# ViT block on one core: values per token tile through DRAM, masked keys, unrolled attention with block-diagonal values

## What is computed

```
x = layernorm(patches, ln1) ; x = layernorm(x @ W + bias, ln2) + sincos(position)
h = concat(cls_token + cls_pos_embedding, x)                 # [64, 37, 256]
n = layernorm(h) ; q, k, v = split(n @ Wqkv + bqkv)          # 16 heads of 16
q = q * cos + rotate_half(q) * sin ; k likewise
p = softmax(q k^T / 4)                                       # per image and head, 37 x 37
h = h + (p v) @ Wout + bout
h = h + bitlinear(gelu(bitlinear(layernorm(h), W1, b1)), W2, b2)   # ternary W, 8-bit x
```

## Time and profile before

| | |
|---|---|
| median of three runs | 437.57 us (437.26 to 442.9) |
| the profiled execution, whole | 438.09 us |
| its span in the trace | 436.3 us |
| PE busy | 332.6 us (76%) |
| DVE busy | 322.9 us (74%) |
| ACT busy | 225.3 us (52%) |
| POOL busy | 194.4 us (45%) |

### The profile page before, as it was taken

How to read it: one execution, slowest core, us unless ns; L and a number is a source line. 1 busy time by engine, 2 the same in 40 slices (tenths; PEclk the granted TensorE clock), 3 DMA queues, 4 the chain that set the end, 5 groups by cost and what they waited for, 6 DMA issues and landing times.

```text
span 436.3 us, 10037 instructions
## 1 busy us (share of the span) xinstructions
PE 332.6 (76%) x3539; PEld 251.0 (58%) x3548; DVE 322.9 (74%) x775; ACT 225.3 (52%) x398; POOL 194.4 (45%) x291
## 2 busy tenths in 40 slices
PE   0768999999996679889888898864755746757454
PEld 0556777777763268778777787742433434434333
DVE  1555877778766647877777777677999999999962
ACT  2525445555841144555545555624656565656663
POOL 4143655556543544422333234037566665566440
PEclk9969999999999878999999999987789697788785
DMA  8991500000000000000000000000000000000001
GB/s 239 373 382 39 192 2 1 2 0 0 2 1 2 0 2 2 3 0 0 0 0 0 0 0 0 2 1 1 12 14 25 12 24 12 24 12 24 14 25 31
DMA packets 9015, 16.06 MB, mean 37 GB/s; under 512 B 944, under 2 KB 5744, under 8 KB 8992
## 3 DMA queue, kind: packets, MB, share of 16 engines
q1 hardware_dynamic: 7936, 13.59, 9.0%
q10 hardware_dynamic: 1056, 2.18, 1.7%
HBM read 13.34 MB, written 2.42 MB: 36 GB/s over the span
## 4 chain that ended last, share of the span: by engine, by line
PE 45%; DVE 20%; issue 19%; ACT 8%; POOL 4%; DMA 2%; DVEq 1%; ACTq 0%; POOLq 0%
PE ps L332 11%; PE ps L408 7%; PE ps L358 6%; DVE ximg L815 5%; PE ps L322 3%; DVE ximg L836 3%; PE ps L440 3%; DMA qkT<-in_W 2%; PE ps L416 2%; ACT ximg L968 2%; PE ps L427 2%; PE ps L315 2%; DVE hn L805 2%; PE ps L366 2%; DVE ximg L846 2%
## 5 line engine op out<-in xcount | busy, mean ns | idle before, releaser
L1047 POOL TENSOR_TENSOR rs<-rs,nhalf 128x1 f32<-128x1 f32 (+1 forms) x76 | 42.0, 559 | 102.4 <-DVE rs L621 51.1
L332 PE MATMUL ps<-w_in,xT 128*128 128x256 f32 (+1 forms) x228 | 54.7, 391 | 2.9 <-ACT xT L888 2.9
L954 ACT ACTIVATE ximg<-ps,byp 128x222 f32<-128x222 f32 x64 | 25.0, 443 | 57.6 <-PE ps L448 51.5
L1131 POOL TENSOR_TENSOR ximg<-ximg,wide 128x1024 f32<-128x1024 f32 (+1 forms) x19 | 45.0, 2366 | 21.4 <-ACT ximg L1003 21.4
L332 PEld LDWEIGHTS ps<-w_in,xT 128*128 128x128 f32 (+1 forms) x228 | 42.6, 193 | 10.4 <-ACT xT L888 4.2
L1091 POOL TENSOR_TENSOR ximg<-qkT,ones_c 128x148 f32<-128x148 f32 x32 | 13.8, 432 | 77.7 <-PE ps L402 76.7
L408 PE MATMUL ps<-hnT,w_v 128*128 (+1 forms) x256 | 37.1, 290 | 13.3 <-ACT ximg L968 8.0
L756 DVE TENSOR_TENSOR ximg<-ps,tab 111x512 f32<-111x512 f32 x32 | 22.1, 690 | 30.8 <-PE ps L427 30.8
L408 PEld LDWEIGHTS ps<-hnT,w_v 128*128 128x128 f32 x256 | 32.6, 199 | 18.5 <-issue 17.1
L358 PE MATMUL ps<-w_qk,hnT 128*128 128x512 f32 (+1 forms) x76 | 37.6, 619 | 6.7 <-DVE qb L672 6.7
L500 PE MATMUL ps<-identb,ximg 128*128 128x128 bf16 (+1 forms) x38 | 6.2, 252 | 39.3 <-DVE ximg L836 39.3
(11 more groups left out here) (110 smaller groups left out, 883.6 us busy)
## 6 DMA issues: line engine op xcount, KB each, us to landing
ximg<-in_x SPq DMA_DIRECT2D x18, 384.0 KB, 14.7
out<-ximg SPq DMA_DIRECT2D x18, 128.0 KB, 1.7
ximg<-in_W SPq DMA_DIRECT2D x2, 1024.0 KB, 6.2
wide<-in_rows ACTq DMA_DIRECT2D x1, 768.0 KB, 13.0
w_qk<-in_Wqk SPq DMA_DIRECT2D x1, 512.0 KB, 13.6
qkT<-in_offsets ACTq DMA_DIRECT2D x1, 448.0 KB, 11.0
qkT<-in_W SPq DMA_DIRECT2D x1, 384.0 KB, 5.5
qkT<-in_W ACTq DMA_DIRECT2D x1, 384.0 KB, 9.1
```

Source lines behind the costliest of these rows:

```text
L332: pe.matmul(dst[0:n, :], xT[t % 2][:, k, 0:n], w_in[:, k, :], start=(k == 0), stop=False)
L954: ins = act.activation(vds[u][:, m, :, :].rearrange("p i (r t) -> p i r t", r=3), src, ACT.Identity, bias=b_v[:, m:m + 1])
L1047: pool.tensor_tensor(rs[u][0:n, i:i + 1], rs[u][0:n, i:i + 1], nhalf[0:n, :], ALU.pow).then_inc(S[done], 1)
L1131: pool.tensor_tensor(hd[u][0:n, :], hd[u][0:n, :], fb1[0:n, :], ALU.add).then_inc(S["f_bias"], 1)
```

## The change

The values of a token tile are made in the patch stage (value_product, 128 x 256 a tile), evicted by ACT with a column of ones beside each head, and stored by SP to a DRAM tensor, vsc. When all 19 tiles are there, SP loads them back, two DMAs for each pair, four pairs ahead, onto 48 partitions at 0 and at 64: the even head's values on the lower rows, the odd head's on the upper, both images side by side. What is not loaded was zeroed by POOL once, so each block of 101 rows by 34 columns is block-diagonal over two heads. Probabilities are stored with 64 columns for each head, so that one transpose turns two heads (101 x 101), eight a pair instead of six. The product takes 16 matmuls of 34 columns instead of 12 of 51 or 17. The values' bias goes once through w_o into the offset row (out_offset, at the start). Keys are masked when ACT evicts them, in three instructions for q and the two masked copies of k, so POOL's copies for each pair go, and the scores read the canvas. hnT shrinks to two tile buffers. Attention's PSUM banks are laid out anew (probabilities in 4 and 5, the output in 6 and 7), and its order is written out for all 35 steps on every engine.

```diff
+            sp.dma_start(w_o[:], a["Wo"].rearrange("(k p) n -> p k n", p=128)).then_inc(S["ld_o"], 16)
...
+            sp.dma_start(w_v[:], a["Wv"].rearrange("(k p) n -> p k n", p=128)).then_inc(S["ld_v"], 16)
...
+            def store_values(t):
+                n = 128 if t < NT else RL + 16
+                sp.wait_ge(S["v_evac"], t + 1)
+                sp.dma_start(vsc[128 * t:128 * t + n, :], vt[t % 2][0:n, :, :, :].rearrange("p e g c -> p (e g c)")
+                             ).then_inc(S[f"v_stored{t % 2}"], 16)
+
+            def load_values(p):
+
+                if p < 4:
+                    sp.wait_ge(S["v_zero"], 1)
+                else:
+                    sp.wait_ge(S["o_ready"], p - 3)
+                for e in range(2):
+                    src = bass.AP(vsc.tensor, PW * p * VROW + e * HC * VW,
+                                  [[VROW, 48], [TOK * VROW, 2], [1, HC * VW]])
+                    sp.dma_start(vb[p % 4][64 * e:64 * e + 48, :, e, :], src).then_inc(S[f"vb{p % 4}"], 16)
+
+            for t in range(NT + 1):
+                store_values(t)
...
+            sp.wait_ge(S["v_stored0"], 16 * (NT // 2 + 1))
+            sp.wait_ge(S["v_stored1"], 16 * (NT // 2))
+            for p in range(NP):
+                load_values(p)
...
+            def out_offset():
+                pe.wait_ge(S["ld_o"], 16)
+                for k in range(2):
+                    mm = pe.matmul(ps[0:K3, 5, 0:D], bass.AP(byp, 2 * KP + k, [[2 * KP + 2, 128], [0, K3]]),
+                                   w_o[:, k, :], start=(k == 0), stop=(k == 1))
+                mm.then_inc(S["orow"], 1)
...
+            def value_product(t):
+                pe.wait_ge(S["h_canvas"], t + 1)
+                war(pe, "v_evac", t, 1)
+                if t == 0:
+                    pe.wait_ge(S["ld_v"], 16)
+                n = rows(t)
+                for k in range(2):
+                    mm = pe.matmul(ps_v[0:n, :], hnT[t % 2][:, k, 0:n], w_v[:, k, :], start=(k == 0), stop=(k == 1))
+                mm.then_inc(S["v_ready"], 1)
...
+                    value_product(s - 4)
...
+            def scores(p):
+                pe.wait_ge(S["qk_canvas"], tiles_of(p))
...
+                            at0 = PW * p + TOK * i
+                            rhs = bass.AP(qkT, qkT[32 * r:32 * r + 32, 2 + c, at0:at0 + TOK].offset,
+                                          [[6 * COLS, 32], [2 * COLS, 2], [1, TOK]])
+                            dst = ps[64 * i:64 * i + TOK, r, 2 * TOK * c:2 * TOK * c + 2 * TOK]
+                            mm = pe.matmul(dst.rearrange("p (e t) -> p e t", e=2),
+                                           qkT[32 * r:32 * r + 32, c, at0:at0 + TOK], rhs, start=True, stop=True)
                 mm.then_inc(S["s_ready"], 1)
...
-            def values(p, u):
-                for m in range(2):
-                    for k in range(2):
-                        mm = pe.matmul(ps_v[:, m, :], w_v[:, k, 128 * m:128 * m + 128],
-                                       hnT[:, k, bass.ds(PW * p, PW)], start=(k == 0), stop=(k == 1))
-                return mm
...
+            def turn_probs(p, b):
                 pe.wait_ge(S["s_exp"], p + 1)
-                war(pe, "p_evac", p, 1)
...
-            def turn_values(p, u):
-                pe.wait_ge(S["v_evac"], p + 1)
-                war(pe, "v_block", p, 1)
-                for i in range(2):
...
+                war(pe, f"p_evac{b}", p, 1)
+                for g in range(4):
+                    at0 = 2 * 64 * (4 * (b - 4) + g)
+                    flat = pr[p % 2][0:SPAN, :, :].rearrange("p h t -> p (h t)")
+                    mm = pe.transpose(ps[0:SPAN, b, SPAN * g:SPAN * g + SPAN], flat[:, at0:at0 + SPAN],
+                                      ident[0:SPAN, 0:SPAN])
+                mm.then_inc(S[f"p_turned{b}"], 1)
+
+            def turn_out(p, b):
+
+                pe.wait_ge(S["o_norm"], p + 1)
+                pe.wait_ge(S[f"p_evac{b}"], min(p + 2, NP))
+                war(pe, "o_canvas4" if b == 4 else "o_canvas", p, 1)
+                m = b - 4
+                pe.transpose(ps[:, b, O_AT:O_AT + SPAN], at[p % 4][0:SPAN, 128 * m:128 * m + 128],
+                             ident[0:SPAN, 0:SPAN]).then_inc(S[f"o_turned{b}"], 1)
+
+            def attend(p):
+                pe.wait_ge(S["p_evac4"], p + 1)
+                pe.wait_ge(S["p_evac5"], p + 1)
+                pe.wait_ge(S[f"vb{p % 4}"], 32 * (p // 4 + 1))
+                war(pe, "o_norm", p)
+                for g in range(HC):
                     for i in range(2):
-                        mm = pe.matmul(ps[64 * i:64 * i + TOK, 7, 3 * VW * g:3 * VW * g + n],
-                                       pT[u][0:k, g, 64 * i:64 * i + TOK],
-                                       vbd[u][0:k, i, 3 * VW * g:3 * VW * g + n], start=True, stop=True)
+                        rhs = vb[p % 4][0:SPAN, i, :, VW * g:VW * g + VW]
+                        dst = ps[64 * i:64 * i + TOK, 6 + p % 2, 2 * VW * g:2 * VW * g + 2 * VW]
+                        mm = pe.matmul(dst.rearrange("p (e c) -> p e c", e=2), pT[p % 2][0:SPAN, g, i, :], rhs,
+                                       start=True, stop=True)
                 mm.then_inc(S["o_ready"], 1)
...
+            def attention_step(s):
+                if live(s, NP) and s > 0:
+                    scores(s)
+                if live(s - 3, NP):
+                    turn_out(s - 3, 5)
+                    turn_out(s - 3, 4)
+                if live(s - 2, NP):
+                    attend(s - 2)
                 if live(s - 1, NP):
-                    pe.wait_ge(S["v_evac"], s)
-                    pe.wait_ge(S["s_exp"], s)
-                if live(s - 2, NP):
-                    pe.wait_ge(S["p5_evac"], s - 1)
-                if live(s - 4, NP):
-                    pe.wait_ge(S["o_canvas"], s - 3)
-                if live(s, NP):
-                    mm = values(s, u)
-                if live(s - 1, NP):
-                    mm = turn_last_probs(s - 1, 1 - u)
-                if live(s - 3, NP):
-                    mm = turn_out(s - 3, 1 - u)
-                mm.then_inc(S["bank5"], 1)
-                if live(s - 1, NP):
-                    turn_probs(s - 1, 1 - u)
...
+            pe.wait_ge(S["a_init"], 2)
+            for s in range(NP + 1):
+                attention_step(s)
...
+            v.wait_ge(S["orow"], 1)
+            v.tensor_tensor(qko[:, 2 * D:3 * D], ps[0:K3, 5, 0:D], qko[:, 2 * D:3 * D], ALU.add).then_inc(S["bmix"], 1)
...
-            v.memset(ps[:, 0:4, :], 1.0)
-            v.memset(ps[:, 7, :], 1.0)
-            for u in range(2):
-                v.tensor_copy(vbd[u][:, :, :].rearrange("p i (h c) -> p i h c", c=VW)[:, :, :, HD],
-                              tab[:, vmask_o:vmask_o + NH].unsqueeze(1).to_broadcast([128, 2, NH])
-                              ).then_inc(S["a_init"], 1)
+            v.memset(ps[:, 0:4, 0:4 * TOK], 1.0).then_inc(S["a_init"], 1)
...
-            def place_values(p, u):
-                v.wait_ge(S["v_turned"], p + 1)
-                war(v, "o_ready", p)
-                m = tab[0:V3, vmask_o:vmask_o + NH]
-                v.tensor_tensor(vbd[u][0:V3, :, :].rearrange("p i (h c) -> p i h c", c=VW)[:, :, :, 0:HD],
-                                ps_vT[0:V3, :].rearrange("p (i h c) -> p i h c", i=2, c=HD),
-                                bass.AP(m.tensor, m.offset, [[NTAB, V3], [0, 2], [1, NH], [0, HD]]), ALU.mult
-                                ).then_inc(S["v_block"], 1)
...
+            v.wait_ge(S["v_zero"], 1)
+            attention_step(0)
+            v.wait_ge(S["qk_canvas"], NT + 1)
+            v.memset(ps[:, 6:8, 0:NH * VW], 1.0).then_inc(S["a_init"], 1)
...
+            def values_out(t):
+                act.wait_ge(S["v_ready"], t + 1)
...
+                else:
+                    act.wait_ge(S[f"v_stored{t % 2}"], 16 * (t // 2))
+                n = rows(t)
+                act.activation(vt[t % 2][0:n, :, :, 0:HD],
+                               ps_v[0:n, :].rearrange("p (g e d) -> p e g d", e=2, d=HD), ACT.Copy
+                               ).then_inc(S["v_evac"], 1)
 
             def qk_out(t):
                 act.wait_ge(S["qk_turned"], t + 1)
-                to_canvas(qkT, ps_qkT, t, "qk_canvas")
+                if t == 0:
+                    act.wait_ge(S["b_done"], 2)
+                n = rows(t)
+                at0 = 128 * t
+                act.activation(qkT[:, 0:2, at0:at0 + n], ps_qkT[:, 0:2, 0:n], ACT.Copy)
+                for e in range(2):
+                    ins = act.activation(qkT[:, 2 + 2 * e:4 + 2 * e, at0:at0 + n], ps_qkT[:, 2:4, 0:n], ACT.Copy,
+                                         scale=tab[:, pmask_o + e:pmask_o + e + 1])
+                ins.then_inc(S["qk_canvas"], 1)
...
+                if live(s - 5, NT + 1):
+                    values_out(s - 5)
...
-            def values_out(p, u):
-                war(act, "v_turned", p)
```

(51 more changed lines are left out.)

194 lines of the change are left out of this document (72 added, 122 removed).

## The result

| | before | after |
|---|---|---|
| median of four runs | 439.69 us | 463.1 us (461.41 to 465.45) |
| ratio, 95% interval | | 1.053 (1.043 to 1.063) |
| profiled execution, its span | 438.09, 436.3 us | 465.45, 463.6 us |
| scores of pair 1 | 156.54 | 173.16 |
| scores of pair 1 to those of pair 31 | 120.9 us | 128.65 us |

A forecast was written before the change was run, and what follows sets the result against it. It took PE to bound the patch stage and, with short waits, attention. 438.1 + 1.5 + 14.6 + 0.6 + 0 - 28.8 - 1.2 = 424.8, about 424.5 for the median; range 412 to 440, 8 in 10.

The forecast's parts named there:

- What bounds each stage: Patch stage: PE alone, 6.08 us a tile; attention: PE's work plus short waits; feed-forward: DVE busy 38.35 of 40 us.
- Start, +1.5: Kernel start: the new addition on DVE and ACT's cut of the row delay tile 1's statistics by 1.5 us.
- Patch stage, +14.6 and +0.6: Patch stage: values add 0.86 us a tile on PE for 17 tiles, +14.6; at the stage's end +0.6.
- POOL's fills, 0: End of patch stage: POOL's fills of 4224 columns cost nothing on the path; upper bound a slip of about 4 us.
- The DMAs: Storing and reloading values before attention: hidden, or up to 2 us late; later loads have four steps, 11 us, for 1.7.
- Attention, -28.8: Attention, scores of pair 1 to those of pair 31: 92.1 us in place of 120.9.
- the tail: Last scores to last normalisation, 9.3 us before: two rounds get about 0.6 shorter, -1.2.
- I give three steps to that clock: Attention's entry: three steps run at the low clock, 4.2 us each, before 27 steps of 2.9.
- the rival: Attention, all steps: idle time before attend keeps PE at 1.2 GHz, 27 steps cost 4.2, +35, so 460; chance 0.12.
- The low-clock step, 4.2: Attention step at the low clock: transposes 1.6, ACT's evictions 0.81, attend 1.6 and waits 0.2 make 4.2 us.
- The step at 2.4 GHz, 2.9: Attention step at full clock: transposes 0.91, ACT's evictions 0.81, attend 1.01 and semaphore waits make 2.9 us.
- the 92.1 forecast: Attention, pair 1 to pair 31: 3 x 4.2 + 27 x 2.9 + 1.2 for w2's pieces = 92.1 us.

The follow-up runs named there:

- the runs with 60.00 of 60 us busy at 0.50: Changed kernel with four matmuls of 128x128 weights and 74 dense columns added behind the scores of each attention step; 505.91 us, ratio 1.149.
- 451.78 us: Changed kernel with only the output transposes moved into free columns of the output banks, no transposes added; 451.78 us, ratio 1.021.
- 476.0 us: Changed kernel, no added work, but in steps 2 to 8 PE waits for the normalisation of the pair just attended; 476.0 us.
- the second filler: Changed kernel with eight 128x128 float32 transposes added behind the scores of each attention step; 428.98 us, ratio 0.975.
- 445.92 us: Changed kernel with eight 128x128 transposes added in each of the attention steps 17 to 24 only; 445.92 us.
- the run of 429.31 us: Changed kernel with four plain float32 matmuls per step, 128 columns of the identity moving, not marked as transposes; 429.31 us.

## Why the prediction was wrong, step by step

- **What bounds each stage.** Right: 6.94 a tile in the patch stage, feed-forward only shifted (149.2 for 149.6).
- **Start, +1.5.** In the pair of profiles tile 1's statistics began at 23.29 for 20.37, +2.9. One pair isn't a fair measure here. The next row of DVE's statistics of this kind (2.3 us behind) began at 22.65, 23.84 and 22.97 in the three kernels with the old start (mean 23.15), and at 23.73 to 26.96 in the fourteen with the new one (mean 25.11): +2.0. Of that, 0.5 is in the arrival of W (PE's first matmul at 10.72 and 11.24 on average), which leaves 1.4.
- **Patch stage, +14.6 and +0.6.** 0.86 a tile, as worked out. The scores of pair 1 came 16.6 later, my terms gave 16.7.
- **POOL's fills, 0.** The lower end was right: 2.02 for 4 x 544 columns and 1.84 for 2 x 1024, 3.9 us in all. The sum behind them started at 165.19, 0.1 us after its operands were ready, as in the kernel before; nothing waits for the fills.

```profile
161.42 2.02 POOL L1128 MEMSET ximg<- 128x544 f32 x4
163.38 1.84 POOL L1130 MEMSET ximg<- 128x1024 f32 x2
```

- **The DMAs.** Right: 1.9 us to landing for a load, 1.7 for a store, and PE waits for none of them in attention.
- **Attention, -28.8.** This step failed; it measured +7.8, and the tail +3.4 for -1.2. Together they are 41.2 us off, and the whole forecast is 38.6 off (40.7 for the profiled execution, 465.45 against 424.8). The failing sentence is "I give three steps to that clock": the fall at the entry came as it says, the way back didn't, and the thirty steps from pair 1 to pair 31 took 128.65 us, 4.3 each. It took the recovery from the old kernel, which had its value transposes to recover with, and the change removes just those. The same slip stands behind the line against the rival, "the loop, in which PE was idle for 10.3 of 96 us, had 1.00 throughout": I judged by PE's idle time, and the runs with 60.00 of 60 us busy at 0.50 show that it tells nothing of this.
- **The rival's reason.** Its price came out near (4.2 a step and 460 us; 4.39 and 463.1 were measured), its reason did not. It named the half microsecond of idle time ahead of attend. Without this wait the clock was 0.50 too (451.78 us), and with more waiting it was no different (476.0 us).
- **The low-clock step, 4.2.** 4.39, so near in part by luck: the output transposes on the loop (0.50, left out) and attend, 1.16 from start to start for the forecast's 1.6, nearly cancel.
- **The step at 2.4 GHz, 2.9.** 3.06, from two errors that nearly cancel: the 0.36 of the output transposes was left out and ACT took 0.94 for 0.81, but attend took 0.70 from start to start, not 1.01: its instructions of 34 columns follow each other in 0.022 us where the old ones, most of 51, took 0.032, and I had kept the old figure. With loads of 37 columns in both, the measured 22 ns lies below each of the two figures that the prediction quotes from the Trainium skill for them, 30.8 and about 25; that 31.7 agreed with the first says nothing of attend here. With the clock repaired by transposes in eight steps, pair 1 to pair 31 took 265.73 - 172.11 = 93.6 us for the 92.1 forecast, and the whole 425.83 for 424.5. So for a clock that the change took away the sum holds, part of it because these errors offset.

I can't say what the chip counts, nor why the step of the changed kernel is enough to keep 2.4 GHz and not enough to get it. What is shown is which added and removed work moved the level in this kernel, and that the same steps ran at either level.

The Trainium skill, "TensorE: Matmul & The Clock Gate", section "Part 4: PE-mode transpose", says that the full clock does not engage for transposes. By that, an estimate from this case's rows, the eight of the second filler would have made the step 1.3 us longer at 1.2 GHz (they take 1.65 there, and PE's wait of 0.36 covers some), and the time about 503 us; 428.98 us at 2.4 GHz was measured. The same page of the Trainium skill, section "Why this matters for your kernels", advises keeping TensorE busy without long gaps to raise the clock and to hold it. Here that was not sufficient: 60.00 of 60 us busy at 0.50.

## What to carry to other kernels

Before you take work off TensorE, see what brings the clock back at the stage's entry: here it was the four transposes of the values, which looked like pure cost. Price a stage at both clocks and look at the granted clock before you look at any wait; where a stage of small matmuls stays at 1.2 GHz although PE is always busy, try a few transposes into unused columns in its first steps: here eight of them cost about 0.9 us in each of eight steps, and the whole was 37 us shorter all the same. And when a transposed result shares a bank with something that is being evicted, look whether its wait for the bank lies on the loop; here it did, though its own data had long been there.

## What the runs showed of the hardware

- Steps with the same instructions ran for tens of us at either level: 0.50 in the steps 2 to 16 and 1.00 in the steps 25 to 31 of one execution (445.92 us).
- The changed kernel with float32 blocks of 128x128 and 128 moving columns added was granted 1.00, with dense values or the identity, marked as transposes or not (428.98, 426.56, 429.31, 432.23 us); with 74 moving columns 0.50, dense or identity (505.91, 505.74 us).
- PE can be busy all the time at either level: 60.00 of 60 us at 0.50 (505.91 us) and 59.99 at 1.00 (428.98 us).
- A float32 transpose of 128x128 takes 0.12 us from start to start at 2.4 GHz (232.05 - 231.12 for eight), and each of the two instructions of a float32 matmul with 128 columns 0.13 (1.00 for eight, in the run of 429.31 us).
- GpSimd fills a column of 128 float32 in 0.9 ns (1024 in 0.92 us), against 2.37 us for adding 1024.
